# Last output stage of a four-layer triangle-product network: stage and final turn made into one, by pairs of tiles

## The reference

```python
xn = _layernorm(x, norm_scale, norm_bias)
left = (xn @ W_left + b_left) * mask * sigmoid(xn @ W_lgate + b_lgate)
right = (xn @ W_right + b_right) * mask * sigmoid(xn @ W_rgate + b_rgate)
out_gate = sigmoid(xn @ W_ogate + b_ogate)
out = einsum('bikd,bjkd->bijd', left, right)
out = _layernorm(out, out_norm_scale, out_norm_bias) * out_gate
return out @ W_out + b_out          # and x = x + this, the program's output
```

## Time and profile before

| | us |
|---|---|
| median of three runs | 1943.2 |
| lowest, highest | 1935.28, 1946.1 |
| the profiled execution, its own time | 1933.59 |
| its span, first to last instruction | 1931.8 |
| `mix` of layer 3 and the fold of its sums end | 1749.7 |
| `finish` of layer 3: first load issued to the last addition | 1750.2 to 1882.9 |
| `leave`: first turn to the end | 1883.2 to 1931.8 |

### The profile page before, as it was taken

One profiled execution on the slowest core, in us unless ns is written; L12 is line 12 of the kernel. 1 busy time (PEld: TensorE's weight loads), 2 busy tenths in 40 slices (PEclk: granted clock), 3 DMA queues, 4 the chain that ended last, 5 costly groups with the idle time before them and its releaser, 6 DMA issues. The chain is left out here.

```text
span 1931.8 us, 29873 instructions
## 1 busy us (share of the span) xinstructions
PE 1538.0 (80%) x7296; PEld 758.3 (39%) x7296; DVE 1331.0 (69%) x2126; ACT 882.9 (46%) x1446; POOL 265.5 (14%) x224
## 2 busy tenths in 40 slices
PE   5597498966586576999979995667999967766998
PEld 4445233211275122222239992222222235652447
DVE  3884499067588696377757776993577757767994
ACT  3795343833234244766646662005666634440003
POOL 0000087000000484100000001661100000000000
PEclk8998799999898798999989997998999989997999
DMA  5667410035567440098889995870388879976759
GB/s 201 212 132 220 128 47 13 5 108 142 157 214 261 100 89 3 11 309 280 279 274 299 304 302 183 289 280 1 129 288 279 282 250 307 309 252 228 273 211 348
DMA packets 253817, 386.36 MB, mean 200 GB/s; under 512 B 24227, under 2 KB 165414, under 8 KB 244262
## 3 DMA queue, kind: packets, MB, share of 16 engines
q1 hardware_dynamic: 205718, 337.35, 54.2%
q10 hardware_dynamic: 48016, 47.98, 7.5%
HBM read 193.74 MB, written 190.32 MB: 199 GB/s over the span
## 5 line engine op out<-in xcount | busy, mean ns | idle before, releaser
L993 PE MATMUL bank<-work 128*128 128x256 f32 x1408 | 346.8, 394 | 59.0 <-ACT work L1025 31.8
L719 ACT ACTIVATE work<-bank,bias 128x512 f32<-128x512 f32 x448 | 276.9, 686 | 210.8 <-PE bank L617 135.4
L1345 POOL TENSOR_TENSOR xT<-xT,work 128x512 f32 (+1 forms) x192 | 241.9, 1270 | 846.6 <-DVE work L1399 846.5
L784 DVE SCALAR_TENSOR_TENSOR work<-bank,bias,work 128x512 f32<-128x512 f32 x320 | 228.4, 747 | 138.3 <-PE bank L650 94.7
L993 PEld LDWEIGHTS bank<-work 128*128 128x128 f32 x1408 | 265.1, 197 | 113.6 <-issue 23.2
L650 PE MATMUL bank<-work,w 64*128 64x512 f32 x1024 | 268.8, 627 | 5.4 <-DVE work L784 4.0
L1018 ACT COPY work<-bank 128x512 f32<-128x512 f32 x176 | 103.2, 586 | 230.0 <-PE bank L993 129.1
L706 ACT ACTIVATE work<-bank,fold 128x512 f32<-128x512 f32 x192 | 116.7, 689 | 190.3 <-PE bank L617 190.0
L1284 PE MATMUL bank<-work,w 128*128 128x512 f32 (+2 forms) x512 | 193.3, 612 | 1.3 <-DVE work L1362 1.3
L1273 PE MATMUL bank<-work,sel 128*128 128x512 bf16 x176 | 70.1, 403 | 151.0 <-DMA work<-rstd_parts 98.2
L1082 DVE TENSOR_TENSOR work<-work 128x512 f32<-128x512 f32 x176 | 121.2, 689 | 70.8 <-ACT work L1018 70.1
(11 more groups left out here) (131 smaller groups left out, 1834.7 us busy)
## 6 DMA issues: line engine op xcount, KB each, us to landing
work<-hidden_rows SPq DMA_DIRECT2D x352, 256.0 KB, 3.6
hidden_rows<-work SPq DMA_DIRECT2D x288, 256.0 KB, 2.2
z_rows<-work ACTq DMA_DIRECT2D x176, 256.0 KB, 3.6
work<-z_rows SPq DMA_DIRECT2D x32, 1024.0 KB
work<-gate_rows SPq DMA_DIRECT2D x32, 1024.0 KB, 4.8
work<-in_x SPq DMA_DIRECT2D x64, 256.0 KB, 3.9
hidden_rows<-work SPq DMA_DIRECT2D x128, 128.0 KB, 2.3
gate_rows<-work SPq DMA_DIRECT2D x64, 256.0 KB, 2.4
```

The source lines that it names most:

```text
L719: nc.scalar.activation(result(tile, column), GB[(NG * j + n) % len(GB)][:, :], ACT.Sigmoid, bias=bias(name)).then_inc(gate_sb, 1)
L784: dve.scalar_tensor_tensor(out=r, in0=VB[(NV * j + m) % len(VB)][:, :], scalar=bias(value_w), in1=r, op0=ALU.add, op1=ALU.mult).then_inc(v ...
L993: mm = pe.matmul(ZB[b % 2][:, r * N:r * N + N], a[:, kk, r * P:r * P + P], x[:, kk, :], start=(kk == 0), stop=(kk == 1))
L1345: pool.tensor_tensor(x, x, term[:, ring(j, q, TERMS), :], ALU.add).then_inc(x_sb, 1)
```

## The change

- `finish(core, 3, 1, None)` and `leave(core)` are replaced by one stage, `finish_out(core)`. It works by 32 pairs of tiles (1024 pixels).
- Per pair PE has two selection products, four 64x64 quarter products with "zc", four with "wout" (both by `two_tiles`, in which the odd tile's halves change places and change back), and the eight turns of the pair three before; the columns that a turn reads lie 8 elements apart.
- DVE keeps two passes a tile (z times 1/std, and bias and gate). ScalarE adds the output bias (an Identity activation into `term`), GpSimd adds that to x, and ScalarE makes both copies of the turned pieces and issues the two stores of a pair, of 256 KB each, as before in bytes.
- z and gate are loaded by pairs, 512 KB each, into three buffers; the 1/std parts in four groups of three DMAs (before: 16 groups). All parts of the stage have a place of their own in SBUF, so its memset covers 4 x 512 bf16 columns, before 2 x 512.
- In layer 3 `project` stores an odd tile's gate with its halves exchanged, in one DMA of 256 KB rather than two of 128 KB.
- The stage is written out with no loop, on all engines.

```diff
-    stores = (NG, NG + 1)
+    swap_gate = layer == 2
+    stores = (NG, NG if layer == 3 else NG + 1)
...
-                    swapped(core.gate_d, result(k, 0))
+                    if swap_gate:
+                        swapped(core.gate_d, result(k, 0))
+                    else:
+                        sp.dma_start(core.gate_d[:, ds(at, T)], result(k, 0)).then_inc(stored[k], 16)
...
-def leave(core):
+def finish_out(core):
...
+    TERMS, RES, IN = 6, 4, 3
+    FAC, GB, OB, TR = bank[0:2], bank[2:4], bank[4:6], bank[6:8]
...
+    dst = core.out.rearrange("a (h p) (n k) c -> h (a p n) (k c)", h=2, k=KC)
...
+        @block.sync
+        def _(sp):
+            def load(u):
+                b = u % IN
+                at_least(sp, cen_mm, 2 * (u - IN) + 2)
+                sp.dma_start(z[:, b, :, :].rearrange("p j t -> p (j t)"),
+                             core.z_d[:, u * 2 * T:u * 2 * T + 2 * T]).then_inc(landed[b], 16)
+                at_least(sp, term_sb, 2 * (u - IN) + 2)
+                sp.dma_start(gate[:, b, :, :].rearrange("p j t -> p (j t)"),
+                             core.gate_d[:, u * 2 * T:u * 2 * T + 2 * T]).then_inc(gates_in[b], 16)
...
+            sp.wait_ge(zeroed, 1)
+            load_parts(0)
+            for u in range(IN):
+                load(u)
+            for q in range(1, NT // JP):
+                load_parts(q)
+            for u in range(IN, PAIRS):
+                load(u)
...
+            def factors(u):
+                q, j = 2 * u // JP, 2 * u % JP
+                if j == 0:
+                    pe.wait_ge(parts_in[q], 16 * 3)
+                at_least(pe, zn_sb, 2 * u)
...
+            def centre(u):
+                pe.wait_ge(zn_sb, 2 * u + 2)
+                at_least(pe, term_sb, 2 * u)
+                two_tiles(GB, w("zc"), [z[:, u % IN, n, :] for n in range(2)], cen_mm)
+
+            def out(u):
+                pe.wait_ge(term_sb, 2 * u + 2)
+                at_least(pe, y_sb, 2 * u)
+                two_tiles(OB, w("wout"), [term[:, (2 * u + n) % TERMS, :] for n in range(2)], out_mm)
+
+            def turn(u):
+                pe.wait_ge(x_sb, 2 * u + 2)
                 for half in range(2):
+                    at_least(pe, kept, 2 * (u - 1) + half + 1)
                     for k in range(4):
+                        first = u * 2 * T + 4 * half + k
+                        mm = pe.transpose(TR[half][:, k * P:(k + 1) * P], xT[:, first:(u + 1) * 2 * T:KC],
+                                          core.ident[:, :])
+                    mm.then_inc(turn_mm, 1)
+
+            factors(0)
+            for u in range(PAIRS + 3):
+                if u + 1 < PAIRS:
+                    factors(u + 1)
+                if u < PAIRS:
+                    centre(u)
+                if 1 <= u <= PAIRS:
+                    out(u - 1)
+                if u >= 3:
+                    turn(u - 3)
...
+            def biased(u):
+                for t in (2 * u, 2 * u + 1):
+                    act.wait_ge(out_mm, t + 1)
+                    nc.scalar.activation(term[:, t % TERMS, :], OB[t % 2][:, :], ACT.Identity,
+                                         bias=vec("b_out")).then_inc(y_sb, 1)
+
+            def keep(u):
+                r = u % RES
+                at_least(act, stored[r], 32 * (u // RES))
+                to = res[:, r, :].rearrange("p (h k c) -> p h k c", h=2, k=KC)
+                for half in range(2):
+                    act.wait_ge(turn_mm, 2 * u + half + 1)
+                    nc.scalar.copy(to[:, :, 4 * half:4 * half + 4, :],
+                                   TR[half][:, :].rearrange("p (k h c) -> p h k c", k=4, h=2)).then_inc(kept, 1)
+                act.wait_ge(kept, 2 * u + 2)
+                for h in range(2):
+                    act.dma_start(dst[h, u * P:u * P + P, :], res[:, r, h * KC * C:(h + 1) * KC * C]
+                                  ).then_inc(stored[r], 16)
+
+            for u in range(1, PAIRS + 3):
+                if u <= PAIRS:
+                    biased(u - 1)
+                if u >= 3:
+                    keep(u - 3)
...
+        @block.gpsimd
+        def _(pool):
+            for t in range(NT):
+                x = xT[:, t * T:t * T + T]
+                pool.wait_ge(y_sb, t + 1)
+                pool.tensor_tensor(x, x, term[:, t % TERMS, :], ALU.add).then_inc(x_sb, 1)
...
+            def normed(u):
+                dve.wait_ge(landed[u % IN], 16 * (u // IN) + 16)
+                for n in range(2):
+                    zt = z[:, u % IN, n, :]
+                    dve.wait_ge(fac_mm, 2 * u + n + 1)
+                    dve.tensor_tensor(zt, FAC[n][:, :], zt, ALU.mult).then_inc(zn_sb, 1)
+
+            def gated(u):
+                dve.wait_ge(gates_in[u % IN], 16 * (u // IN) + 16)
+                for n in range(2):
+                    t = 2 * u + n
+                    dve.wait_ge(cen_mm, t + 1)
+                    at_least(dve, x_sb, t - TERMS + 1)
+                    dve.scalar_tensor_tensor(out=term[:, t % TERMS, :], in0=GB[n][:, :], scalar=vec("out_norm_bias"),
+                                             in1=gate[:, u % IN, n, :], op0=ALU.add, op1=ALU.mult).then_inc(term_sb, 1)
+
+            dve.memset(parts, 0.0).then_inc(zeroed, 1)
+            normed(0)
+            for u in range(PAIRS):
+                if u + 1 < PAIRS:
+                    normed(u + 1)
+                gated(u)
```

More of the change, by code:

```diff
@@ L1413, in _, with load_parts @@
                     statistics(g, j, q)
-def leave(core):
-    nc, bank = core.nc, core.bank
+def finish_out(core):
+    nc, bank, xT = core.nc, core.bank, core.xT
     KC = 8
[L1420 to L1430, removed]
-    with ExitStack() as ctx:
-        turned, kept_a, kept_v = core.sems("leave", "turned kept_a kept_v")
-        stored = core.sems("leave", "st0 st1 st2 st3")
-        kept = [kept_a, kept_v]
-        block = ctx.enter_context(nc.Block())
+    PAIRS = NT // 2
+    TERMS, RES, IN = 6, 4, 3
+    FAC, GB, OB, TR = bank[0:2], bank[2:4], bank[4:6], bank[6:8]
+    z, at = core.area([IN, 2, T], 0)
+    gate, at = core.area([IN, 2, T], at)
+    parts, at = core.area([NT // JP, T], at, BF16)
+    term, at = core.area([TERMS, T], at)
+    res, at = core.area([RES, 2 * KC * C], at)
+    w = lambda name: core.w[:, SLOT[name], :]
+    vec = lambda name: core.vec[:, VEC[name]:VEC[name] + 1]
+    lower, upper = slice(0, C), slice(C, 2 * C)
+    dst = core.out.rearrange("a (h p) (n k) c -> h (a p n) (k c)", h=2, k=KC)
+    with ExitStack() as ctx:
+        (fac_mm, zn_sb, cen_mm, term_sb, out_mm, y_sb, x_sb, turn_mm, kept, zeroed) = core.sems(
+            "last", "fac_mm zn_sb cen_mm term_sb out_mm y_sb x_sb turn_mm kept zeroed")
+        parts_in = core.sems("last", "parts0 parts1 parts2 parts3")
+        landed = core.sems("last", "in0 in1 in2")
+        gates_in = core.sems("last", "gate0 gate1 gate2")
+        stored = core.sems("last", "st0 st1 st2 st3")
+        block = ctx.enter_context(nc.Block())
+        @block.sync
[8 more added lines that the diff above has]
+                             core.gate_d[:, u * 2 * T:u * 2 * T + 2 * T]).then_inc(gates_in[b], 16)
+            def load_parts(q):
+                for n in range(3):
+                    src = core.rstd_d[n:n + 1, :].rearrange("a (h s t) -> s (a h) t", h=2, t=T)
+                    sp.dma_start(parts[32 * n:32 * n + 32, q, :], src[JP * q:JP * q + JP, :, :]).then_inc(parts_in[q], 16)
+            sp.wait_ge(zeroed, 1)
[6 more added lines that the diff above has]
+                load(u)
@@ L1438, in _, with two_tiles @@
         @block.tensor
         def _(pe):
-            for n in range(stores):
+            def two_tiles(outs, weights, movings, made):
+                for out, x, first, second in ((outs[0], movings[0], lower, upper), (outs[1], movings[1], upper, lower)):
+                    pe.matmul(out[first, :], weights[lower, lower], x[lower, :], start=True, stop=True)
+                    pe.matmul(out[second, :], weights[upper, upper], x[upper, :], start=True,
+                              stop=True).then_inc(made, 1)
@@ new lines, in _ @@
+            for u in range(1, PAIRS + 3):
[3 more added lines that the diff above has]
+                    keep(u - 3)
+            for r in range(RES):
+                act.wait_ge(stored[r], 32 * (PAIRS // RES))
+        @block.gpsimd
[4 more added lines that the diff above has]
+                pool.tensor_tensor(x, x, term[:, t % TERMS, :], ALU.add).then_inc(x_sb, 1)
@@ L1513, in build @@
         fold_sums(core, 3, 64, mask, sums)
-        finish(core, 3, 1, None)
-        leave(core)
+        finish_out(core)
 def kernel(**inputs):
```

20 lines of the change are left out of this document (3 added, 17 removed).

## The result

The changed kernel takes 1891.7 us (median of four runs, 1890.96 to 1902.71) against 1941.4 us before, measured beside it; the ratio is 0.9758 with a 95% interval of 0.9722 to 0.9793, so 2.4% faster. Applied to the 1943.2 us of the front table the ratio gives 1896 us; the forecast was 1906, with a range of 1893 to 1930. The profiled execution has a span of 1889.2 us, 42.6 less than before; 37.4 were forecast.

What follows compares the result with a forecast made beforehand. The DMA engines were to bound the fused stage: 132.1 us of bytes from 1753.7, 1.5 of coupling and 7.1 of end chain gave 1894.4 against 1931.8; 37.4 off 1943.2 made 1906 us, range 1893 to 1930.

Steps and rivals of the forecast that it cites:

- The rate of the bytes: New stage: loads at 385 GB/s and stores at 382, 132.1 us in all or 4.13 us a pair.
- Rival (b): New stage: loads and stores together get only the rate of `mix`, 156.5 us, whole 1930; chance 0.16.
- The start: Start of the new stage: first z load issued at 1752.9, bytes flowing from about 1753.7, DVE beginning at 1756.8.
- The coupling: SyncE's queue in the new stage: gate loads waiting ahead of z loads cost 0.05 us a pair, 1.5 us.
- The end: Chain behind the last gate load: 12.6 us, of which 7.1 us come on top of the DMA sum.
- (d): New stage better than forecast: loads at 410 and a faster mixture, or engines at 3.7 to 3.9 us a pair; 1893 to 1899; chance 0.10.
- (a): New stage bound by the DMA engines as forecast: 1906, by itself 1899 to 1917; chance 0.52.
- (c): New stage paced by waits, late z loads or PE, not bytes: 4.6 us a pair, 1928; chance 0.14.
- (g): Transfers don't overlap within a queue: 64 loads take 230 us, about 2000 for the median; chance 0.02.
- (e): Quarter products on PE overlap only two by two: 5.3 us a pair, 1950 or no change; chance 0.03.
- (f): TensorE falls to 1.2 GHz in the new stage: 6.6 us a pair, 1993 for the median; chance 0.03.
- The gate store in `project`: In `project`, 64 stores of 128 KB become 32 of 256 KB: 0 us, bound 1 us either way.

Runs made afterwards that it cites:

- the last run: Fifteen unread fp32 products on TensorE, added to the changed kernel with four z buffers, early first z load, spread parts loads and shared end: 1890.0 us, ratio 0.9752.

## Why the prediction came out as it did

**The mechanism was right.** The bound went from PE and DVE to the DMA engines, with the engines' work beside it. The share and DVE's waits say so; the fourth buffer, which lengthened the queue and not the rate, and the gate's loads, without which the pair shortened until PE was full, show it. It holds for the middle; the start, below, went at the engines' pace. From DVE's first pass (1756.30) to the end there were 132.9 us, where 138 were forecast.

**The rate of the bytes was sized too low.** I took 385 for loads and 382 for stores, 4.13 us a pair; the middle ran at 412, 3.8 us. By itself that makes 50.7 MB / 412 = 123.1 us rather than 132.1, 9 us less. The stores' 382 was exact. The term that was mis-sized is the interpolated rate of loads, with the rule that both kinds together get what each gets alone (4 KB loads alone run at 410, and with stores the two make 415, not 400). The interpolation was weak at one end: it stood on loads of 2 KB rows that ran at 316 with a share of 0.94 in the first stage, "so 336 if full", and 2 KB rows, though of another array, reach 381 when queued. Dividing a rate by its share does not give the full rate; a share of 0.94 there, 0.96 in `mix` and 0.98 without the gate all stood at rates well below what the blocks of queued DMAs reach with rows of the same size. Rival (b) fell with the same division: `mix` is not held by its rows or its mixture, which reach 384. What its loads wait for is the likely limit; no run changed it.

**The start was sized too short.** I let the full rate begin at 1753.7. From 1753 to 1763 and from 1763 to 1773 the DMA engines moved 353 and 356 GB/s, before any store (the first is issued at 1772.27), and 376 in the next 10 us, when stores had begun. At 412 from 1753.7 on, 13.6 MB would have moved by 1786.8; 12.8 had: 2 us. My sum had taken the bytes as the bound from the first load on. But loads alone are 1.049 MB a pair, and from 1769 to 1779 the z loads were 3.40 us apart, PE's pace: that is 308 GB/s until the stores join. PE set the pace there, and the bytes only later. Ahead of 1769 the clock was low for 11 us and SyncE issued nine loads of parts (5.7 us); what each of them costs was not told apart.

**The coupling.** I charged 0.05 us a pair, 1.5 us, because a z load has some 5.6 us to land and was to take 3.6. It took 7.4, and DVE waited for it in nearly every pair of the middle, 1.2 us each time. With the DMA engines full meanwhile, that wait is the bytes themselves and costs nothing beside them.

**The end.** From the start of the last gating it took 14.0 us where I had 12.6, and the rate had begun to fall before it: 375 GB/s from 1860 to 1875.

**Together** the end came at 1889.2 instead of 1894.4. The rate alone would have put it 9 us earlier and the missing coupling 1.5 more; 2 us of the start, 1.4 of the last chain and some 2 more, which I take to be the falling rate ahead of it, hid half of that. That 1906 lies as near as it does is in part luck: a rate too low met a start and an end too short. By the prediction's own list what came is (d), loads at 410 and a faster mixture, 1893 to 1899 with a chance of 0.10, since (a) by itself reached down to 1899 only; the bound is the one of (a). (c) is out by the DMA share of 1.04, and (g) because z loads that took 7.4 us to land were 3.77 us apart.

**PE.** 3.6 us a pair was forecast and 3.4 measured, where PE was full for want of gate loads: turns with columns 8 apart cost 0.88 for eight, the lower bound, not the 1.1 taken. Quarters overlap by four as the earlier trace rows showed, so (e) is out; whole products make 4.74. The clock stood at 1.00 through the middle with PE busy 26 to 28 of 30 us, so (f) is out.

**DVE and GpSimd.** I used DVE's durations (2.84 us for four passes). The DVE-only sum had six passes in 3.75 to 3.82 us, where durations add to 4.3: a pass starts before the one before has ended, by some 0.1 us (two passes on z take 1.29 us in the timeline, at a mean of 0.686 each). GpSimd's price was right (1.276 us), and so was ScalarE's bias pass, for which I had no row: 0.684 us, where 0.686 was taken.

**Where the gain of 42 us comes from**, by taking one part of the change back at a time: without the quarters 29 of it go, without the fusing 26, without GpSimd's sum 2. They add to more than 42: without the quarters alone, PE is the bound of the one long stage, and without the fusing alone, the stage of stores is back, so each needs the other for its full worth.

**The gate store in `project`.** I took 0 with a bound of 1 us. The stage's first mask load came at 1559.51 before and 1560.30 after, from nearly the same start (hidden_rows stores at 1384.88 and 1384.87): 0.8 us later, so within the bound and no gain.

**The Trainium skill's rule of size** ("DMA: Bandwidth & Descriptors", section "Bandwidth": 1 MiB or more for 75% of peak, 341 GB/s measured there at 1 MB with DMAs issued from GpSimd) did not hold for transfers that stand in line: 512 KB loads with 256 KB stores ran at 412 in the kernel and 415 in a block of DMAs alone. The 425 GB/s that the Trainium skill has in the same table for a load of 16 MB is near the 424 found here for 1 MiB loads in rows of 8 KB.

## What to carry to other kernels

When two stages that follow each other have different limits, compute the bytes and each engine's work of both together; here that gave the bound, and the sum needed both the fusing and less work on PE. Price bytes with transfers that are really queued: a window's rate divided by its DMA share understates what the engines can do, and a short block of queued DMAs of the right row size is the better price. Look at the start of a stage apart from its middle: before the stores began, it ran some 14% under the rate of the middle (353 and 356 against 412), and at least from 1769 on it was PE and not the bytes that set the pace there. One more buffer took 4.6 us off the stage of 142, about half of it by the start.

## What the runs showed of the hardware

- Queued loads on one core (nine blocks of DMAs alone, one profile): 424 GB/s in rows of 8 KB, 410 in 4 KB, 381 in 2 KB, 349 in 1 KB. Queued stores in 2 KB rows: 382, side by side or 64 KB apart.
- Loads of 4 KB rows with stores of 2 KB rows (2 to 1 in bytes, on two queues) together: 415, more than either alone. 1 KB both ways: 384, more than 1 KB loads alone.
- Turns of fp32 128x128 pieces cost 0.11 us each with columns 8 elements apart (eight in 0.88 us, the run with whole products), as with columns side by side (0.87), and 0.15 with columns 256 apart.
- TensorE at 2.4 GHz (granted clock 1.00) fell to 1.2 GHz (0.50) behind a stretch of 3 us in which it worked 0.54 us, though it had worked 2.70 of the 3 us before (the last run).
- Four 64x64 fp32 products with 512 columns ran at once, 0.43 us a step (the run without gate loads): a pair's four such steps took 1.88 us to the next turn, where eight steps of whole products took 3.43.
